# Relu attention with the score matmuls of two heads interleaved, one PSUM bank for the projection and a bf16 normalizer row

## The reference

```python
qkv = (x @ w_qkv).reshape(Bx, Sx, H, 3 * HD)
scores = einsum('bhqd,bhkd->bhqk', q, k) / sqrt(HD)
w = relu(scores)
attn = w / (sum(w, axis=-1, keepdims=True) + 1e-6)
out = einsum('bhqk,bhkd->bhqd', attn, v)
out = out.reshape(B, S, D) @ w_out + b_out
y = x + out
s = (y - mean(y)) * rsqrt(var(y) + 1e-5) * gamma + beta
```

## Time and profile before

| | us |
|---|---|
| median of 2 runs | 6270.05 |
| lowest and highest run | 6266.88, 6273.23 |
| the profiled execution, its own time | 6315.74 |
| its span on core 1, the slowest | 6314.2 |
| spans of cores 0 to 3 | 6297.7, 6314.2, 6277.4, 6296.2 |
| spans of cores 4 to 7 | 6278.1, 6265.0, 6277.6, 6264.9 |

### The profile page before, as it was taken

One profiled execution on the slowest core, in us unless ns is written; L12 is line 12 of the kernel. 1 busy time (PEld: TensorE's weight loads), 2 busy tenths in 40 slices (PEclk: granted clock), 3 DMA queues, 4 the chain that ended last, 5 costly groups with the idle time before them and its releaser, 6 DMA issues.

```text
span 6314.2 us, 41696 instructions; the slowest of 8 cores (6264.9 to 6314.2 us)
## 1 busy us (share of the span) xinstructions
PE 3208.6 (51%) x11072; PEld 1133.1 (18%) x11072; DVE 2260.7 (36%) x3909; ACT 898.8 (14%) x1807; POOL 540.3 (9%) x391
## 2 busy tenths in 40 slices
PE   0977677677677434233332198845233333078970
PEld 0411111111111111111110043311011111033330
DVE  0344344344344246344442111126444443111112
ACT  2011111111111101011111110001011111210100
POOL 0000100100100100000002222110000000321210
PEclk9955555555555567555555599967555555587785
DMA  6310000000000240200000384640200000183634
GB/s 175 38 27 1 10 17 0 27 0 0 27 0 0 60 67 0 60 0 1 0 0 33 67 80 52 75 87 0 60 0 1 0 0 19 39 90 50 60 61 146
DMA packets 384005, 226.75 MB, mean 36 GB/s; under 512 B 323138, under 2 KB 339522, under 8 KB 383778
## 3 DMA queue, kind: packets, MB, share of 16 engines
q0 software_dynamic: 226096, 92.98, 12.9%
q1 hardware_dynamic: 128882, 59.79, 4.4%
q10 hardware_dynamic: 28800, 71.32, 3.3%
HBM read 220.54 MB, written 50.33 MB: 43 GB/s over the span
## 4 chain that ended last, share of the span: by engine, by line
PE 42%; DVE 24%; DMA 9%; issue 8%; ACT 7%; SPq 4%; POOL 3%; ACTq 1%; DVEq 1%; POOLq 0%
PE psum L1184 10%; PE psum L591 9%; PE psum L573 9%; PE psum L1235 5%; ACT arena L945 3%; DVE arena L612 3%; DMA arena<-arena 3%; DVE arena L936 3%; DVE arena L939 3%; PE psum L986 3%; PE psum L925 2%; DMA arena<-w_f 2%; DVE arena L972 2%; SPq L726 2%; PE psum L460 2%
## 5 line engine op out<-in xcount | busy, mean ns | idle before, releaser
L1184 PE MATMUL psum<-arena 128*128 128x512 bf16 (+1 forms) x2816 | 659.6, 401 | 534.3 <-DMA arena<-w1a_f 534.3
L986 PE MATMUL psum<-arena 128*64 128x128 bf16 x1120 | 165.4, 308 | 1033.1 <-DVE arena L972 1033.1
L591 PE MATMUL psum<-arena 128*65 128x512 bf16 x1024 | 627.3, 631 | 85.0 <-DVE arena L582 83.0
L573 PE MATMUL psum<-arena 64*128 64x512 bf16 x1024 | 574.3, 586 | 125.4 <-DVE arena L502 1.0
L582 DVE TENSOR_SCALAR arena<-psum 128x512 bf16<-128x512 f32 x512 | 354.2, 692 | 762.0 <-PE psum L573 748.5
L586 ACT ACTIVATE arena<-psum 128x512 bf16<-128x512 f32 x512 | 306.0, 598 | 1538.1 <-PE psum L573 1531.8
L786 PE MATMUL psum<-arena 128*128 128x512 bf16 x768 | 259.5, 509 | 414.0 <-DVE arena L794 143.3
L1184 PEld LDWEIGHTS psum<-arena 128*128 128x128 bf16 (+1 forms) x2816 | 287.2, 102 | 906.7 <-issue 679.1
L945 ACT ACTIVATE arena<-arena 128x640 bf16<-128x640 f32 (+4 forms) x256 | 194.7, 761 | 1376.2 <-DVE arena L941 1376.2
L1235 PE MATMUL psum<-arena 128*128 128x512 bf16 x1408 | 337.5, 407 | 94.6 <-DMA arena<-w_f 91.5
L1204 DVE SCALAR_TENSOR_TENSOR arena<-psum,arena 128x1024 bf16<-128x1024 f32 x88 | 113.0, 1284 | 653.0 <-ACT arena L1198 653.0
(11 more groups left out here) (118 smaller groups left out, 2794.9 us busy)
## 6 DMA issues: line engine op xcount, KB each, us to landing
arena<-w_f POOLq DMA_DIRECT2D x8, 2816.0 KB, 18.0
arena<-w1a_f POOLq DMA_DIRECT2D x84, 256.0 KB, 4.5
arena<-w1g_f POOLq DMA_DIRECT2D x84, 256.0 KB, 4.6
arena<-x ACTq DMA_DIRECT2D x32, 512.0 KB, 5.0
arena<-scr_xn ACTq DMA_DIRECT2D x32, 512.0 KB, 9.8
scr_xn<-arena ACTq DMA_DIRECT2D x16, 512.0 KB, 14.5
scr_tp<-arena POOLq DMA_DIRECT2D x32, 256.0 KB, 16.0
scr_s<-arena SPq DMA_DIRECT2D x16, 512.0 KB
```

The costliest lines, as they stand in the source:

```text
L573: ev_mm = r.op("tensor", lambda e, kc=kc, kp=kp, t=t, sp=sp, c=c: e.matmul(ps_sc[sp][:, 0:512], kT3[kp:kp + 64, kc, t * 128:(t + 1) * 128] ...
L591: r.op("tensor", lambda e, h=h, t=t, sp=sp, up=up: e.matmul(ps_u[up][0:65, 0:512], va3[:, t, 65 * h:65 * h + 65], ws3[:, sp, :], start=(t ...
L986: r.op("tensor", lambda e, h=h, kt=kt, j=j, par=par, wmax=wmax: e.matmul(ps_o[par][0:64, 0:128], v3[:, kt, 64 * h:64 * h + 64], atT3[:, pa ...
L1184: r.op("tensor", lambda e, sgrp=sgrp, k=k, nch=nch, psAG=psAG, scol=scol, rows=rows: e.matmul(psAG[0:rows, nch * 512:(nch + 1) * 512], w1b ...
```

## The change

The loop over 16 heads becomes a loop over 8 pairs of heads, `hp`. There are now four score banks and four buffers in `wst`, two for each head of the pair (`sp = hh * 2 + t % 2`). Per key tile PE does the AV of both heads and then the scores of both heads two tiles ahead. The tile goes to DVE when t + hh is even, else to ACT. After the last tile the normalizers of both heads follow one after the other. The bank for this comes from the projection: `at` is one bank, and each row tile is done in two halves of 512 columns, each with its own wait for DVE and its own bias add. `rr` becomes bf16.

```diff
-        ps_sc = [self.P.alloc(f"sc{i}", 1) for i in range(3)]
+        ps_sc = [self.P.alloc(f"sc{i}", 1) for i in range(4)]
-        ps_at = self.P.alloc("at", 2)
+        ps_at = self.P.alloc("at", 1)
-        rr = self.alloc("rr", 512, F32)
+        rr = self.alloc("rr", 512, BF16)
...
-            for h in range(HA):
-                kc, kp = h // 2, (h % 2) * 64
-                up = h % 2
-                r.wait("tensor", u_guard[up])
+            for hp in range(8):
+                kc = hp
+                r.wait("tensor", u_guard[0])
+                r.wait("tensor", u_guard[1])
...
-                def emit_scores(t, sp):
+                def emit_scores(hh, t):
+                    sp = hh * 2 + t % 2
+                    kp = hh * 64
                     r.wait("tensor", sc_guard[sp])
...
-                    eng = "vector" if t % 2 == 0 else "scalar"
+                    eng = "vector" if (t + hh) % 2 == 0 else "scalar"
...
-                emit_scores(0, 0)
-                emit_scores(1, 1)
+                for hh in range(2):
+                    emit_scores(hh, 0)
+                for hh in range(2):
+                    emit_scores(hh, 1)
                 for t in range(NT):
+                    for hh in range(2):
+                        emit_av(hh, t)
                     if t + 2 < NT:
-                        emit_scores(t + 2, (t + 2) % 3)
-                    emit_av(t, t % 3)
-                u_done = r.marker("tE")
+                        for hh in range(2):
+                            emit_scores(hh, t + 2)
+                for hh in range(2):
+                    u_done = r.marker("tE")
...
             for t in range(4):
                 stile = 4 * c + t
-                r.wait("tensor", at_guard)
-                for k in range(KT):
-                    for nch in range(2):
+                for nch in range(2):
+                    r.wait("tensor", at_guard)
+                    for k in range(KT):
...
-                r.wait("vector", yw_guard)
-                at_guard = r.op("vector", lambda e: e.scalar_tensor_tensor(
-                    yw[:, 0:D], ps_at[:, 0:1024], 1.0, boutv[:, 0:D],
-                    ALU.mult, ALU.add), inc="vE")
+                    if nch == 0:
+                        r.wait("vector", yw_guard)
+                    at_guard = r.op("vector", lambda e, nch=nch: e.scalar_tensor_tensor(
+                        yw[:, nch * 512:(nch + 1) * 512], ps_at[:, 0:512], 1.0,
+                        boutv[:, nch * 512:(nch + 1) * 512],
+                        ALU.mult, ALU.add), inc="vE")
```

More of the change, by code:

```diff
@@ L581, in emit_scores @@
                     if eng == "vector":
-                        ev_evs[t] = r.op("vector", lambda e, sp=sp: e.tensor_scalar(
+                        ev_evs[hh][t] = r.op("vector", lambda e, sp=sp: e.tensor_scalar(
                             ws3[:, sp, :], ps_sc[sp][:, 0:512], 0.0, None,
@@ L604, in p1 @@
-                u_done = r.marker("tE")
[L605 to L608, removed]
-                with_lp = self.nc.allow_low_precision
-                def _recip(e):
-                    with with_lp("bf16 normalizer is a matmul operand"):
-                        return e.reciprocal(rrb[64:65, 0:512], rr[64:65, 0:512])
@@ L613, in p1 @@
-                ev_r = r.op("vector", _recip, inc="vE")
-                u_guard[up] = r.op("vector", lambda e, up=up: e.tensor_copy(
-                    ub[0:64, 0:512], ps_u[up][0:64, 0:512]), inc="vE")
-                r.wait("tensor", ev_r)
-                r.wait("tensor", bc_guard)
-                ev_bc = r.op("tensor", lambda e: e.matmul(
-                    ps_bc[0:64, 0:512], ones64v[64:65, 0:64],
-                    rrb[64:65, 0:512], start=True, stop=True), inc="tE")
-                rr_guard = ev_bc
@@ L622, in p1, with _radd, _recip @@
-                r.wait("vector", ev_bc)
-                dsto = oT4[:, ob, h // 2, :][kp:kp + 64, :]
-                bc_guard = r.op("vector", lambda e, dsto=dsto: e.tensor_tensor(
-                    dsto, ub[0:64, 0:512], ps_bc[0:64, 0:512], ALU.mult), inc="vE")
+                        for hh in range(2):
+                            emit_scores(hh, t + 2)
+                with_lp = self.nc.allow_low_precision
+                for hh in range(2):
+                    u_done = r.marker("tE")
+                    kp = hh * 64
+                    r.wait("vector", u_done)
+                    r.wait("vector", rr_guard)
+                    def _radd(e, hh=hh):
+                        with with_lp("bf16 normalizer is a matmul operand"):
+                            return e.tensor_scalar(
+                                rr[64:65, 0:512], ps_u[hh][64:65, 0:512], 1e-6,
+                                None, ALU.add)
+                    r.op("vector", _radd)
+                    def _recip(e):
+                        with with_lp("bf16 normalizer is a matmul operand"):
+                            return e.reciprocal(rrb[64:65, 0:512], rr[64:65, 0:512])
+                    ev_r = r.op("vector", _recip, inc="vE")
+                    u_guard[hh] = r.op("vector", lambda e, hh=hh: e.tensor_copy(
+                        ub[0:64, 0:512], ps_u[hh][0:64, 0:512]), inc="vE")
+                    r.wait("tensor", ev_r)
+                    r.wait("tensor", bc_guard)
+                    ev_bc = r.op("tensor", lambda e: e.matmul(
+                        ps_bc[0:64, 0:512], ones64v[64:65, 0:64],
+                        rrb[64:65, 0:512], start=True, stop=True), inc="tE")
+                    rr_guard = ev_bc
+                    r.wait("vector", ev_bc)
+                    dsto = oT4[:, ob, kc, :][kp:kp + 64, :]
+                    bc_guard = r.op("vector", lambda e, dsto=dsto: e.tensor_tensor(
+                        dsto, ub[0:64, 0:512], ps_bc[0:64, 0:512], ALU.mult),
+                        inc="vE")
@@ L697, in p1 @@
         r.fence()
-        for i in range(3):
+        for i in range(4):
             self.P.free(f"sc{i}")
```

32 lines of the change are left out of this document (17 added, 15 removed).

## The result

| | before | after |
|---|---|---|
| median, us | 6282.45 (10 runs) | 5868.55 (11 runs) |
| lowest and highest run, us | 6266.88, 6387.81 | 5854.45, 6052.88 |
| ratio after to before | | 0.9355 [0.932, 0.939] |
| the profiled execution, its own time | 6315.74 | 5849.06 |
| spans of the 8 cores in it | 6264.9 to 6314.2 | 5805.8 to 5847.5 |

The changed kernel is faster by 6.1 to 6.8%. That is some 405 us by the ratio and 414 by the medians. The forecast was 5945 with 325 us saved, so its direction and its range (5630 to 6060) hold and the saving came out some 85 us larger. The narrower range that it gave for a head loop at 1.2 GHz throughout, 5900 to 6000, was missed by some 30 us.

What follows compares the result with a forecast made beforehand. The prediction took PE to bound the head loop, waiting once per key tile on its own AV's semaphore. Four chunks gain 339 us, the projection costs 14, so 6270-325 = 5945 us; range 5630 to 6060.

Steps and rivals of the forecast that it cites:

- if the clock leaves 0.50 in the loop: Head loop: a sign that the forecast is wrong; TensorE's granted clock was to stay at 0.50, 1.2 GHz.
- AV to scores: Step of a head-loop round, from the second AV to the first scores: 0.51 us, taken from the other direction.
- scores to scores: Step of a head-loop round between the two heads' scores: 0.28 to 0.42 us, middle taken, giving a round of 1.80.
- AV to AV: Step of a head-loop round between the two heads' AV matmuls: 0.43 us.
- scores to AV: Step of a head-loop round, from the second scores to the next AV: 0.51 us.
- The end of a pair: After a pair's last AV: both normalizers in turn, second broadcast matmul at 10.31 us, next pair's first AV 2.50 later.
- rr in bf16: Normalizer's reciprocal with a bf16 row: stays at 3.34 us, gain 0; 107 us more if twice as fast.
- The projection: Projection in one bank: 2.1 us more for a chunk's first tile, 0.5 for each other; 14 us in all.
- Rival 1: Head loop: the clock rises to 2.4 GHz, round about 1.05 us, total 5628 us; chance 0.18.
- Rival 2: Head loop: AV to scores takes 0.79 also behind AV(1), round 2.13 us, total 6093 us; chance 0.06.
- Rival 3: Head loop: changing row halves empties the array each time, round 2.80 us, total 6393 us; chance 0.03.
- Rival 4: Head loop: no change, PE finds the same wait elsewhere, round near 2.5 us; chance 0.02.

Runs made afterwards that it cites:

- second experiment: The kernel before with one line moved: a score bank is released by its eviction, not by the AV; 6119.52 us, ratio 0.9701.
- first experiment: The changed kernel with heads h and h+2 paired, so both use the same half of the partitions; 6061.43 us, ratio 0.9568.
- the third: The changed kernel with a score bank released by its eviction instead of by the AV; 5659.56 us, ratio 0.8969.
- fifth experiment: The changed kernel with the normalizer row rr back in float32; 5861.67 us, ratio 0.9332.

## Why the prediction was right, and where its sizes were off

By one of its own signs the prediction was wrong: it names "if the clock leaves 0.50 in the loop", and the clock left it. The total stayed inside the range because the range reached down to the clock case. Two terms of the round were off to opposite sides and cancelled in part: AV to scores took 448 x 0.05 = 22 us more than priced, scores to scores 448 x 0.13 = 58 us less.

**What bounds the loop: right.** The wait of the scores for the AV just ahead was the cost. Moved alone (second experiment) it is worth 162 us of the stretch, with a second head under it (first experiment) 259.

**AV to AV 0.43 and scores to AV 0.51: right.** Both are in the rows to a hundredth.

**AV to scores: 0.51 taken, 0.56 measured.** I used the other direction's row for this one. The second experiment shows the same 0.56 where no semaphore is left.

**Scores to scores: 0.35 taken, 0.22 measured.** This is the term that was mis-sized. The step's lower end was argued as "the second scores wait for AV(1), 0.79 after its start", and that is what happens: 0.56+0.22 = 0.78 after it. Only the split was wrong: of the 0.79 more lies ahead of the first scores and less behind. I put the middle of the two ends into the sum although the lower one came from a wait that I could name and the upper one from a row of three scores on one half. The first experiment is that upper end (0.40, round 1.96), the third shows that nothing but the wait holds the lower one (0.01). By the Trainium skill, "TensorEngine Tiling (Array Packing)", Key Properties, the prediction had the round at 1.73 and the total at 5914; the round measured 1.72. In the sum the term and the one above it make 448 x (1.80-1.725) = 34 us.

**The end of a pair: right.** 10.30 to the second broadcast against 10.31, 2.49 to the first AV against 2.50, idle 9.7 against about 10. With the measured round a pair is 14 x 1.725+1.93+10.31+2.50 = 38.89; pairs without a rise take 38.81.

**rr in bf16 at nothing: right,** shown by the fifth experiment above.

**The projection: 14 us taken, about 9 measured.** The 0.5 per later tile is 0.4. The first tile was to cost 2.1 more and costs 0.8 in the mean (7.96 against 7.16). Where PE did both groups of eight at 1.2 GHz the forecast's 9.3 is met (two chunks of core 2); where the second eight ran at 2.4 GHz (1.89 in place of 3.57) it is 7.59 and 7.44. So "If PE runs the second eight at the full clock, about 3" was the right branch in some chunks and not in others. From the first projection matmul to the next chunk's first AV it is 59.1, 57.1 (988.83 to 1045.95) and 58.8 on core 2, and 57.9 in the mean of the eight cores, where 59 was forecast and 55.7 stood before. (The prediction calls this the way from the last product; its 55.8 starts at the first projection matmul, 735.05.)

**The clock: the forecast's 0.50 was wrong for a fifth of the pairs.** Rival 1 was set up as all or nothing, 5945 against 5628, with one clause that "if it rises only late in some pairs, the time lies between". That clause is what came. 28 x (38.81-37.50) = 37 us in the pairs. Of the three periods that hold a projection (92.8, 95.1, 96.6) the first had a rise too: less its projection (59.1, 57.1, 58.8) it is 33.7 against 38.0 and 37.8, 4 more. The rounds at 2.4 GHz are 1.08 against the rival's 1.05, and a pair that rises early saves 38.81-31.5 = 7.3. What kept the clock low in the other pairs is not settled: the rounds ahead of the rise are the same 1.73 in both kinds. Shown is only that it depends on the rounds: none of 28 pairs on any core with the round at 1.96, and none in the second experiment, where two heads take 2 x 1.10 per key tile; 6 of 28 on core 2 at 1.72, all pairs at 1.53, and all at 1.93 with five matmuls in place of four. The Trainium skill, "TensorE: Matmul & The Clock Gate", Part 1, has the throttled clock as the default that activity releases; the kernel with repeated matmuls agrees with it, being faster by the work that was added.

**The sum.** In the stretch the forecast was 325 plus the 3.6 of the projection that lies behind it, 329. Add 34 for the round, 37 and 4 for the clock, and 3 for three projections that cost 2.6 and not 3.6 on this core: 407, against 1781.6-1373.2 = 408.4. The two profiled executions differ by 466.7, because the phases outside took 4532.6 us before and 4474.3 after. By the medians of all runs the profiled execution of before stood 33 high and that of after 19 low, which leaves 466.7-33-19 = 414.

**The rivals.** Rival 2 (0.79 also behind AV(1)) is refuted by the 0.56. Its round of 2.13 doesn't follow from the prediction's own steps, 0.43+0.79+0.35+0.51 = 2.08, or 2.15 with 0.42; its time of 6093 would be 6070 or 6102, still above the range. Rival 3 (a change between row halves empties the array) is refuted: scores on two halves start 0.22 apart and scores on one half 0.40, and all four steps stayed below 0.57. Rival 4 would have needed a round near 2.5.

## What to carry to other kernels

Where two ends of a range are open and one of them follows from a wait that can be named, the forecast goes there and not to the middle. A matmul that waits for an earlier matmul's semaphore costs 0.2 us more than the change between the two kinds itself: free the PSUM bank by its eviction, which was worth 162 us in the kernel before and 260 in the one after. TensorE's clock is an outcome of the loop, so a rival about it is priced as a share of the stages and not as all or nothing.

## What the runs showed of the hardware that was not expected

- Two matmuls of 64 rows on different halves run wholly side by side when no semaphore lies between: 0.61 for both, 0.60 for one, at 1.2 GHz, and 0.39 for both at 2.4 GHz.
- More work can take less time: 512 added score matmuls lengthened the round from 1.72 to 1.93 at 1.2 GHz and shortened the kernel by 2.4%, through a clock of 0.74 in place of 0.53.
- With the repeated matmul, program order was not start order: PE was given L575, L581, L575, and the second L575, on the other half, started ahead of L581, which needs the half that the first L575 still used. From a window that leaves out the first:

```profile
1009.70 0.58 PE L575 MATMUL psum<-arena 64*128 64x512 bf16 x1
1009.88 0.63 PE L581 MATMUL psum<-arena 64*128 64x512 bf16 x1
```

- The change from AV to scores costs 0.13 more than AV to AV at 1.2 GHz (0.56 against 0.43), and the change back 0.08 to 0.13 more: 0.51 in the kernel after, 0.53 with the guard moved, 0.56 with both heads on one half.
- PE's busy share says little of its clock: 73% busy at 0.53 in the kernel after, 58% busy at 0.76 with the guard moved. A higher clock lowers the busy share by itself.
